# Causal attention of a four-stage kernel: the pieces of a step spread anew, the groups written out, the mask written by TensorE

## The reference, cut to what matters

```python
NH, KVH, HD, EPS, THETA = 32, 4, 128, 1e-05, 10000.0
h = _rmsnorm(hidden_states, ln1_w)
q = (h @ Wq).reshape(B, S, NH, HD)
k = (h @ Wk).reshape(B, S, KVH, HD)
v = (h @ Wv).reshape(B, S, KVH, HD)
q = _rope(q, pos)
k = _rope(k, pos)
k = jnp.repeat(k, NH // KVH, axis=2)      # eight heads share a k and a v
v = jnp.repeat(v, NH // KVH, axis=2)
scores = jnp.einsum('bqhd,bkhd->bhqk', q, k) / jnp.sqrt(jnp.float32(HD))
scores = jnp.where(causal[None, None], scores, jnp.float32(-1000000000.0))
attn = jax.nn.softmax(scores, axis=-1)
o = jnp.einsum('bhqk,bkhd->bqhd', attn, v).reshape(B, S, NH * HD) @ Wo
x = resid + o
```

## Time and profile before

| | us |
|---|---|
| Runs: lowest, median, highest | 1165.66, 1167.24, 1169.96 |
| The profiled execution, its own time | 1166.56 |
| Its span, first to last instruction | 1164.8 |
| PE busy in the span | 1042.5 (89%) |
| DVE, ACT, POOL busy | 809.1, 693.8, 639.1 |
| TensorE clock granted, mean share | 0.955 |

### The profile page before, as it was taken

How to read it: one execution, slowest core, us unless ns; L and a number is a source line. 1 busy time by engine, 2 the same in 40 slices (tenths; PEclk the granted TensorE clock), 3 DMA queues, 4 the chain that set the end, 5 groups by cost and what they waited for, 6 DMA issues and landing times. The chain is left out here.

```text
span 1164.8 us, 22450 instructions
## 1 busy us (share of the span) xinstructions
PE 1042.5 (89%) x6931; PEld 914.2 (78%) x6931; DVE 809.1 (69%) x1860; ACT 693.8 (60%) x1963; POOL 639.1 (55%) x688
## 2 busy tenths in 40 slices
PE   3798987895999679998999899999979999999998
PEld 3577876784555379888998899899968888888887
DVE  6666675627888868887788788888875555555555
ACT  3455643325899568787887788777843334333342
POOL 5234312441778557775767587666633555555553
PEclk9889989897899779999999999999988999999999
DMA  8000000002213020110011000000011111111111
GB/s 250 1 1 1 2 18 16 1 1 75 89 77 133 13 82 2 47 38 4 2 47 38 4 1 2 2 1 1 2 30 42 41 54 41 54 41 46 49 41 50
DMA packets 44100, 41.78 MB, mean 36 GB/s; under 512 B 6160, under 2 KB 40048, under 8 KB 44000
## 3 DMA queue, kind: packets, MB, share of 16 engines
q1 hardware_dynamic: 42384, 39.54, 11.0%
q10 hardware_dynamic: 1616, 0.99, 0.3%
HBM read 39.40 MB, written 1.11 MB: 35 GB/s over the span
## 5 line engine op out<-in xcount | busy, mean ns | idle before, releaser
L1804 POOL TENSOR_TENSOR prob<-prob,rden 128x128 f32<-128x128 f32 (+1 forms) x256 | 124.8, 509 | 80.4 <-DVE rden L1878 80.3
L2163 POOL TENSOR_TENSOR hid_l<-hid,hid_h 128x512 fp32r<-128x512 f32 x66 | 85.6, 1297 | 134.2 <-ACT hid_h L2132 134.2
L2190 DVE TENSOR_TENSOR hid<-psum,silu 128x512 f32<-128x512 f32 x66 | 45.6, 692 | 125.5 <-ACT silu L2130 125.5
L2130 ACT ACTIVATE silu<-psum 128x512 f32<-128x512 f32 x66 | 39.4, 598 | 117.2 <-PE psum L75 117.2
L2182 DVE SCALAR_TENSOR_TENSOR x<-psum,weight,x 128x256 f32<-128x256 f32 x264 | 108.9, 475 | 0.0
L1753 ACT ACTIVATE prob<-psum,neg_max 128x128 f32<-128x128 f32 (+1 forms) x256 | 105.1, 421 | 5.3 <-issue 3.1
L73 PE MATMUL psum<-xt_h,gu_l 128*128 128x512 f32 x264 | 106.7, 404 | 0.3 <-DVE xt_l L161 0.3
L75 PE MATMUL psum<-xt_h,gu_h 128*128 128x512 f32 x264 | 105.2, 398 | 0.0
L74 PE MATMUL psum<-xt_l,gu_h 128*128 128x512 f32 x264 | 104.8, 397 | 0.0
L1294 POOL TENSOR_TENSOR drive<-u,b_all 128x1024 f32<-128x1024 f32 x32 | 75.4, 2359 | 42.5 <-DVE h L1410 20.7
L1787 POOL TENSOR_TENSOR qr<-r_part_a,r_part_b 128x512 f32<-128x512 f32 x64 | 82.9, 1295 | 8.5 <-DVE r_part_b L1838 8.5
(11 more groups left out here) (281 smaller groups left out, 3728.7 us busy)
## 6 DMA issues: line engine op xcount, KB each, us to landing
b_all<-scan_b_rows SPq DMA_DIRECT2D x16, 512.0 KB, 3.8
early<-in_L_ffn_Wq_dram SPq DMA_DIRECT2D x4, 1024.0 KB, 5.5
early<-in_L_ffn_Wo_dram SPq DMA_DIRECT2D x4, 1024.0 KB, 5.8
raw<-in_L_ffn_Wg_dram SPq DMA_DIRECT2D x32, 128.0 KB, 2.2
raw<-in_L_ffn_Wu_dram SPq DMA_DIRECT2D x32, 128.0 KB, 2.3
raw<-in_L_ffn_Wd_dram SPq DMA_DIRECT2D x32, 128.0 KB, 2.3
x<-_attn_hidden_states_dram SPq DMA_DIRECT2D x8, 128.0 KB, 4.5
early<-in_L_ffn_w_up_q_dram SPq DMA_DIRECT2D x1, 1024.0 KB, 7.1
```

The costliest lines, as they stand in the source:

```text
L1804: ins = pool.tensor_tensor(at, at, rden[:, s % 4, i:i + 1].to_broadcast([P, (i + 1) * P]), ALU.mult)
L2163: pool.tensor_tensor(hid_l[:, j, cols], hid[:, c, :], f(hid_h[:, j, cols]), ALU.subtract)\
```

## The change

1. **Mask.** `peak` loses its addition of the mask and the wait for it (semaphore `masked`). `scores` begins with a matmul of the bf16 identity by the bf16 mask into the two masked stretches of the bank (256 columns), and the matmuls of the scores accumulate on it. The mask in SBUF becomes bf16.
2. **Units of q.** Unit j has phase 0 at r = 2j, one step earlier. POOL's part of `split_q` becomes `low_q`, a phase of its own (6), at the head of its step.
3. **k and v.** POOL's sum becomes `sum_k`, at the head of step r = 5. The low part of v becomes `low_v` (DVE), at r = 5 after `rotate`. PE's `turn_k` goes to the end of step r = 5 and also waits for `v_lo`. The copies of the turned k become `split_k`, at r = 6.
4. **Weights.** The q weights come at steps 20, 22, 24, 26.
5. **Loop.** All groups are written out.
6. **Start.** `FIRST` begins with q. The second half's normalisation (`normalise_rest`) comes late in `FIRST`; its transposes, low parts, the residual (two tiles at a time) and the low parts of the output weights of group 0 are spread over steps 0 to 3 (`BETWEEN`). `Norm` takes its rounds in the order 0, 2, 1, 3, so that half 0 has its second root before half 1 has its first.

```diff
-        WHEN = dict(zip((6, 8, 10, 12, 14, 21, 23, 25, 27), KV + O + Q))
+        WHEN = dict(zip((6, 8, 10, 12, 14, 20, 22, 24, 26), KV + O + Q))
...
+                units = {}
+                for j in range(4):
+                    if own if r < 2 * j else more:
+                        to, batch = (gg, b) if r < 2 * j else ahead_b(gg, b + 1)
+                        units[(r - 2 * j) % REP1] = to, 2 * batch + j // 2, j % 2
+                if 6 in units:
+                    yield "low_q", *units[6]
+                if more and r == 5:
+                    yield "sum_k", *ahead_b(gg, b + 1)
                 if own and (not last or n + 1 < STEPS):
                     yield "scores", *at(1)
...
+                if more and r == 6:
+                    yield "split_k", *ahead_b(gg, b + 1)
                 if 5 in units:
                     yield "split_q", *units[5]
...
                 if more and r == 5:
-                    yield "turn_k", *ahead_b(gg, b + 1)
+                    yield "low_v", *ahead_b(gg, b + 1)
...
                 for phase in (1, 0):
                     if phase in units:
                         yield "q", *units[phase], phase
+                if more and r == 5:
+                    yield "turn_k", *ahead_b(gg, b + 1)
                 if not last and s in WHEN:
                     yield "weights", gg + 1, *WHEN[s]
...
+        FIRST = [("q", 0, 0, 0, 0), ("q", 0, 0, 0, 1), ("kv", 0, 0, 0), ("kv", 0, 0, 1), ("rotate", 0, 0, 0, 0),
+                 ("rotate", 0, 0, 0, 1), ("copy_v", 0, 0), ("rotate_k", 0, 0), ("low_v", 0, 0), ("add", 0, 0, 0),
+                 ("sum_k", 0, 0), ("q", 0, 0, 1, 0), ("q", 0, 0, 1, 1), ("turn_k", 0, 0), ("split_q", 0, 0, 0), ("low_q", 0, 0, 0),
+                 ("split_k", 0, 0), ("scores", 0, 0), ("rotate", 0, 0, 1, 0), ("rotate", 0, 0, 1, 1), ("peak", 0, 0),
+                 ("add", 0, 0, 1), ("q", 0, 1, 0, 0), ("q", 0, 1, 0, 1), ("split_q", 0, 0, 1), ("normalise_rest",),
+                 ("rotate", 0, 1, 0, 0), ("rotate", 0, 1, 0, 1), ("q", 0, 1, 1, 0), ("q", 0, 1, 1, 1)]
+        BETWEEN = {0: [("z", 0), ("wo_low", 0), ("turn_rest",), ("wo_low", 1)], 1: [("z", 2), ("low_rest",), ("wo_low", 2)],
+                   2: [("z", 4), ("wo_low", 3)], 3: [("z", 6)]}
...
-            all_of([*FIRST, *schedule(0, 0, 4, False)])
-            with eng.Fori(0, KVH1 - 1) as g:
+            all_of(FIRST)
+            for n in range(4):
+                all_of(schedule(0, n, n + 1, False))
+                all_of(BETWEEN[n])
+            for g in range(KVH1 - 1):
                 all_of(schedule(g, 4, STEPS + 4, False))
...
-                    at = psum[:, SCOREB[s % 2], :].rearrange("p (c n) -> p c n", c=2)[:, :, 0:P]
-                    dve.tensor_tensor(at, at, mask[:].rearrange("p (c n) -> p c n", c=1).to_broadcast([P, 2, P]),
-                                      ALU.add).then_inc(masked, 1)
-                    dve.wait_ge(masked, STEPS * g + (s + 1))
...
                 def turn_k(g, b):
                     pe.wait_ge(k_roped, k_order(g, b) + 1)
+                    pe.wait_ge(v_lo, k_order(g, b) + 1)
...
-                    pe.matmul(first, qr[:, m % 2, h % QB, 0:P], k_0[:, b % 2, :], start=True, stop=True,
+                    pe.matmul(bank.rearrange("p (c n) -> p c n", c=2)[:, :, 0:P], core.ident_bf[:],
+                              mask[:].rearrange("p (c n) -> p c n", c=1).to_broadcast([P, 2, P]), start=True, stop=False,
+                              skip_group_check=True)
+                    pe.matmul(first, qr[:, m % 2, h % QB, 0:P], k_0[:, b % 2, :], start=False, stop=True,
                               skip_group_check=True)
```

More of the change, by code:

```diff
@@ L1527, in causal_attention @@
         q_tables = sb("rope1_q", [P, 2, S], F32)
-        mask = sb("causal", [P, P], F32)
+        mask = sb("causal", [P, P], BF16)
         part_a = sb("r_part_a", [P, 2, QC], F32)
@@ L1714, in _, with turn_rest, residual @@
                 norm.scalar(act, (0,))
-                def norm_rest():
+                def turn_rest():
                     norm.scalar(act, (1,))
+                def residual(first):
                     act.wait_ge(shifted, 1)
-                    for t in range(NT):
+                    for t in (first, first + 1):
                         act.activation(z[:, t, :], core.x[:, t, :], ACT.Identity, bias=shift[:, t:t + 1],
@@ L1764, in values @@
                     act.activation(ot_h[:, s % 2, :], psum[:, PVB, 0:S], ACT.Copy).then_inc(o_hi, 1)
-                run(act, dict(rotate=rotate, split_q=split_q, turn_k=turn_k, copy_v=copy_v, softmax=softmax, turn_probs=turn_probs, values=values,
-                              weights=weights, norm_rest=norm_rest))
+                run(act, dict(rotate=rotate, split_q=split_q, split_k=split_k, copy_v=copy_v, softmax=softmax, turn_probs=turn_probs, values=values,
+                              weights=weights, turn_rest=turn_rest, z=residual))
             @block.gpsimd
@@ L1781, in _, with wo_low @@
                 pool.wait_ge(norm.normed, NT * norm.norms_before + TH)
-                for piece in Q + O:
+                for piece in Q:
                     weights(0, *piece)
+                def wo_low(n):
+                    weights(0, *O[n])
                 def add(g, m, i):
@@ L1788, in add, with low_q @@
                                        part_b[:, i, :], ALU.add).then_inc(q_roped, 1)
-                def split_q(g, m, i):
+                def low_q(g, m, i):
                     pool.wait_ge(q_hi, q_order(g, m, i) + 1)
@@ L1805, in softmax @@
                     ins.then_inc(p_normed, 1)
-                run(pool, dict(add=add, split_q=split_q, rotate_k=rotate_k, softmax=softmax, weights=weights))
+                run(pool, dict(add=add, low_q=low_q, sum_k=sum_k, wo_low=wo_low, softmax=softmax, weights=weights))
             @block.vector
@@ L1838, in rotate, with low_v @@
                         dve.tensor_tensor(b, b, sin, ALU.mult).then_inc(q_parts, 1)
+                def low_v(g, b):
+                    bank = psum[:, KVB, :].rearrange("p (t n) -> p t n", t=2)
+                    dve.tensor_tensor(v_l[:, b % 2, :], bank[:, 0, HD1:], f(v_h[:, b % 2, :]), ALU.subtract)\
+                        .then_inc(v_lo, 1)
                 def rotate_k(g, b):
@@ L1974, in values @@
                     b = s // REP1
+                    if s == 0 and known(g, 1):
+                        norm.ready(pe, 1)
                     pe.wait_ge(p_lo, STEPS * g + (s + 2))
```

68 lines of the change are left out of this document (34 added, 34 removed).

## The result

The changed kernel takes 1158.43 us, median of 22 runs (1151.24 to 1170.51); the kernel before 1167.6, median of 22 runs on the same chips (1160.35 to 1186.87). The ratio, taken from the fast runs alone, is 0.991, with a 95% interval of 0.9884 to 0.9935: faster by 9 to 10 us, which is under 1%. The profiled execution took 1158.87 with a span of 1156.7, against 1166.56 and 1164.8 before. The forecast was 1157.2, range 1143 to 1167, with 0.71 on faster.

The account below looks back on a forecast made before the run. PE was taken to set the pace in the 14 batches; savings of 6.4 there, 2.6 at the start and 1.0 at the end, 10.0 from 1166.56, gave 1156.6, and 0.7 for the median 1157.2 us, range 1143 to 1167.

Parts of the forecast that it names:

- the forecast's sum: Whole kernel: 6.4 us saved in the 14 batches, 2.6 at the start and 1.0 at the end, 10.0 together.
- The length of a batch: Causal attention: 24.98 us without waits, 0.96 for the mask, 1.0 waiting for the turned k, 0.1 small waits: 27.05.
- 8 x 0.12 = 0.96 a batch: PE in causal attention: the mask's added matmul delays the next matmul by 0.12 us in each of eight steps.
- my 0.1: Small waits in a batch, at r = 4 or 5, where DVE is behind with the low part of the output.
- All of it is the loop (4.9) and the weights (3.5); mask and waits cancel, -2.0 on balance: The 14 batches: 6.4 us less, from removed loop turns and moved q weights, less 2.0 for mask and waits.
- The excess over a plain batch: Three batches splitting q weights: 1.17 us longer, since a POOL piece of 1.30 stands before the low part of q.
- The start: First 8 steps: scores 0 about 2.3 us earlier, ACT the limit from step 3 on, 2.6 kept at step 8.
- The loads of group 1: SP's loads start some 20 us later, landing at 441, just ahead of ACT's first need at about 443.
- The end: After the 14 batches: two waits of some 0.7 us for the low part of q go; 1.0 less, between 0 and 2.
- (A): Rival: `low_v` isn't late and the wait for the turned k vanishes, 15 x 1.0 us more saved, 1142; chance 0.16.
- (B): Rival: the mask's matmul doesn't overlap its neighbours and costs 0.28 us a step, 20 us more, 1177; chance 0.08.
- (C): Rival: straight code stalls as the turns did and q weights still hold q's low part, 1165.6 us; chance 0.19.

## Why the forecast held, and where it did not

**What each part did.** The two kernels with one part alone, against the kernel before, and what is left for the new order (us):

| | start to step 8 | 14 batches | end |
|---|---|---|---|
| loop written out alone | -0.1 | -9.4 | 0.0 |
| mask on PE alone | +0.7 | +3.4 | +0.3 |
| the two added | +0.6 | -6.0 | +0.3 |
| the change | -1.9 | -5.9 | -1.0 |
| left for the new order | -2.5 | +0.1 | -1.3 |

The last line is a difference, not a run: no kernel had the new order alone, and it holds only if the parts add, which they do not quite. Taken out of the changed kernel, the mask's matmul gives 7.6 and not 3.4, and what is left (371.60) is 4.1 below the loop written out alone. What two runs show directly is that order and mask together cost 3.5 in the batches once the loop is written out (379.24 for 375.72). In the start's column two traces of the changed kernel differ by 1.0. It isn't the clock, which was 0.94 in the first 8 steps of both: in the second trace one sine product took 2.32 for 0.71 (last section).

By the stage alone, from its first weight copy to the next norm, the change is worth 8.8 us in one trace (459.32 for 468.09) and 7.9 in the other (460.21), for the 10.0 of the forecast's sum. With the loop written out alone it is 9.5 (458.58).

**The length of a batch: 27.05 forecast, 27.02 to 27.18 measured.** From the mask's start at 628.03 the product begins at 2.73 (2.74 forecast), the sum of k is long done, POOL's `q_l` ends at 3.17 (3.3), the product 0.54 behind it (0.55), `v_l` at 3.92 (4.1). PE's wait shows 0.62 idle, and with `rotate_k` and `low_v` behind `values` the step is 0.9 to 1.1 shorter (1.0). With `q_l` out of the way and no weights ahead the product takes its 0.69.

**"8 x 0.12 = 0.96 a batch": the price per matmul right, the sum not.** 0.12 in four steps of eight, almost nothing in the other four. By the run without it the mask's matmul costs 0.55. That the batch came out right in spite of it is luck: some 0.4 to 0.5 more of small delays was there than my 0.1, in the first two steps and the sixth.

**"All of it is the loop (4.9) and the weights (3.5); mask and waits cancel, -2.0 on balance": this step failed, though its sum, 6.4, stood.** Written out, the loop alone gives 9.4 for my 4.9, of which 2.7 lie in the batches with q weights and 1.3 in plain ones. The excess over a plain batch that I took for the price of POOL's weight piece (1.17) is 0.43 once the loop is written out, with the piece still in place, and in the changed kernel the new places of the weights are worth 0.8 in all. On the other side everything but the loop costs 3.5 in the batches, where my sum had it give 1.5 (the 3.5 of the weights less 2.0). So the loop's gain was sized 4.5 too small and that of the rest 5.0 too large; the two errors nearly cancel, and that the sum stood is luck. The mask costs 3.4 by itself, and with it on PE the new order gives nothing in the batches: it exchanged a wait for POOL's sum for one nearly as long for `v_l`. What could have warned were the batches of the last group, 0.3 quicker than the others and outside the loop; I used them to close the sum and did not ask why.

**The start: 2.6 forecast, 1.9 measured (0.9 in the second trace), for a partly wrong reason.** Scores 0 came 2.4 earlier, for 2.3. Steps 0 to 7 then gave nothing more (0.5 lost, for 0.3 gained in the forecast); but I held that ACT's work is the limit from step 3 on, and with the same work in one piece step 8 comes 3 to 4 us later. The loads of group 1 were issued later and did no harm, as forecast:

```profile
435.07 0.37 SPq L1510 DMA_DIRECT2D early<-in_L_ffn_Wk_dram  x1
...
436.51 0.58 SPq L1510 DMA_DIRECT2D early<-in_L_ffn_Wq_dram  x1
```

ACT takes the first piece of k's and v's weights at 445.90 with no idle time before it. **The end**: 1.0 less, as forecast.

**The rivals.** (A), that `low_v` would not be late, did not come about, but its price was right: with `rotate_k` and `low_v` behind `values` the 14 batches take 13.4 less, for 14 x 1.0. That the single run gave 1142.8 for its 1142 is luck, since the same batches came with 1151.83 and 1146.14. (B), 0.28 a mask, fell to the 0.12. (C), that straight code stalls and the weights still hold q, fell: no idle time at steps 36 and 68, and the batch that now has most of the q weights takes 27.17, for 27.02 to 27.11 of its neighbours.

## What to carry to other kernels

Price the loop itself by a batch that runs outside of it: here writing it out alone gave the stage 9.5 us, more than the whole change (8.8), and more than half of what was saved in batches without a turn (2.2 of 4.0) had looked like the cost of something else. When an operation is put ahead of a wait that another releases, follow every input of the waiting instruction, not just the late one: the turned k exchanged one wait of 1 us for another, and moving `rotate_k` and `low_v` behind `values` took both away. And price work for the engine that sets the pace where that engine has no waits left, since waits hide a part of it: the mask on TensorE cost 3.4 us alone and 8.6 once nothing else was late, and DVE, at 85%, carried it without a wait of TensorE in the batches.

## What the runs showed of the hardware

**The stage's start moves with the clock ahead of it.** The work before the stage ended at 391.0 to 402.9 us over the traces, while the 14 batches of the changed kernel repeat within 0.13. The first 391 us of four of them: the kernel before, the changed one, `low_v` early, and `q_l` late; the third number from the end is the granted clock.

```profile
0.00:391.00 391.00, 322.73 (x1838) 246.68 (x1839) 267.40 (x425) 220.60 (x557) 175.77 (x112) 0.92 0.16 50
```

```profile
0.00:391.00 391.00, 324.97 (x1830) 249.17 (x1831) 267.17 (x422) 219.56 (x556) 175.97 (x112) 0.90 0.16 50
```

```profile
0.00:391.00 391.00, 326.68 (x1806) 251.91 (x1807) 260.80 (x417) 213.96 (x538) 174.02 (x112) 0.87 0.16 50
```

```profile
0.00:391.00 391.00, 326.62 (x1803) 252.07 (x1804) 260.38 (x417) 213.35 (x536) 173.57 (x111) 0.88 0.16 50
```

The stage began at 393.45, 395.82, 402.08 and 402.86. Where the mean clock is 0.87 or 0.88 TensorE stood longer at 1.2 GHz in place of 2.4, and the stage began 6 to 9 us later than at 0.90 or 0.92. Over all 14 traces the order is the same: 402.0 to 402.9 at 0.87 or 0.88, 394.0 to 398.8 at 0.90 or 0.91, 391.0 to 393.5 at 0.92 or 0.93. This is as large as the effect of the change, and the reason why a single run's time says little about it and one stage's length much. The experts scatter too, 300.5 to 304.7 us, but not in step with it (304.70 where the stage began at 402.08, 300.52 where at 402.86).

**The hold between DVE and POOL goes both ways**, and the one that began first wins, be it by 0.02 us. A DVE product of 0.69 that begins under an instruction of POOL ends about 0.55 after it: 61 of the 64 sine products of the kernel before began under `q_l` and ended 0.54 to 0.55 after it. POOL's `q_l` of 0.74 takes 1.27 when DVE was first, and ends 0.60 after DVE's product.

**The hold can go on from one instruction of POOL to the next.** This is the same product, in the first batch, first in the profiled execution of the changed kernel, then in its second trace. In both it began 0.16 before the end of a POOL piece of weights, with multiplications and `q_l` queued behind that piece:

```profile
434.88 0.71 DVE L1866 TENSOR_TENSOR r_part_b<-r_part_b,rope_q 128x512 f32<-128x512 f32 x1 [0.91 <-ACT r_part_b L1753]
435.01 1.42 POOL L1828 TENSOR_TENSOR prob<-prob,rden 128x128 f32<-128x128 f32 x2
```

```profile
430.06 2.32 DVE L1866 TENSOR_TENSOR r_part_b<-r_part_b,rope_q 128x512 f32<-128x512 f32 x1 [0.91 <-ACT r_part_b L1753]
430.20 0.96 POOL L1828 TENSOR_TENSOR prob<-prob,rden 128x128 f32<-128x128 f32 x2
431.12 0.71 POOL L1817 TENSOR_TENSOR q_l<-qr,q_h 128x256 fp32r<-128x256 f32 x1
```

In the first the product went next, and POOL's multiplications took 1.42 for 0.96. In the second it was held through all of them and through `q_l`, and ended 0.55 after `q_l`. PE then waited 2.5 for DVE's low part of the output where it had waited 1.0, and step 8 came 1.0 later. What decides between the two isn't shown.
